# Adapter sums folded from two halves into one operand, and three steps of a fused kernel put in another order

## What is computed

```
x = x + einsum('bct,bcd->bdt', x, w0[itok_B_1_198])
x = x + einsum('bct,bcd->bdt', x, w1[itok_B_0_7])
x = x + einsum('bct,bcd->bdt', x, w2[itok_B_0_7]) + bias[itok_B_0_7][:, :, None]
gate = x @ Wg + (x @ Ag[a]) @ Bg[a]
up   = x @ Wu + (x @ Au[a]) @ Bu[a]
h    = silu(gate) * up
x    = x + h @ Wd + (h @ Ad[a]) @ Bd[a]
```

## Time and profile before

| what | us |
|---|---|
| three runs: median (all) | 1291.2 (1290.88, 1291.2, 1292.76) |
| the profiled execution | 1289.79 |
| its span in the trace | 1288.0 |
| PE busy | 1264.9 (98%), 6236 matmuls |
| weight loads (beside PE) | 1046.2 (81%) |
| DVE busy | 936.5 (73%), 1538 instructions |
| ACT busy | 551.6 (43%), 977 |
| POOL busy | 643.7 (50%), 549 |
| DMA moved | 210.10 MB, mean 163 GB/s |

### The profile page before, as it was taken

The page is one execution under the profiler, slowest core; times in us unless marked ns, Lnnn a source line. Parts: engine busy times, 40 slices in busy tenths (PEclk is TensorE's granted clock), DMA queues, the critical chain, the costliest instruction groups (busy, mean ns, idle before and its releaser), DMA issues.

```text
span 1288.0 us, 17929 instructions
## 1 busy us (share of the span) xinstructions
PE 1264.9 (98%) x6236; PEld 1046.2 (81%) x6236; DVE 936.5 (73%) x1538; ACT 551.6 (43%) x977; POOL 643.7 (50%) x549
## 2 busy tenths in 40 slices
PE   9999999999999999999999999999999999999998
PEld 7788788888888888888888888888888888888886
DVE  7986677777687676777768667767767877676765
ACT  4644445443344344454434444444443433443331
POOL 3465555455535556644545545555553444334443
PEclk9999999999999999999999999999999999999999
DMA  6855444555965345435677434545477643232424
GB/s 202 284 185 183 139 142 133 156 156 170 368 196 172 105 132 144 145 114 155 228 300 225 154 107 151 143 132 155 143 272 259 202 115 91 72 90 93 115 66 131
DMA packets 141047, 210.10 MB, mean 163 GB/s; under 512 B 43424, under 2 KB 87712, under 8 KB 140960
## 3 DMA queue, kind: packets, MB, share of 16 engines
q1 hardware_dynamic: 118656, 138.07, 34.5%
q0 software_dynamic: 22016, 70.80, 17.4%
q10 hardware_dynamic: 288, 0.10, 0.0%
HBM read 164.89 MB, written 44.04 MB: 162 GB/s over the span
## 4 chain that ended last, share of the span: by engine, by line
PE 79%; POOL 11%; issue 4%; DVE 2%; DMA 2%; ACT 0%; SPq 0%; POOLq 0%; DVEq 0%; ACTq 0%
PE px L1519 25%; PE pd L1519 20%; PE py L1519 14%; POOL b_got L658 7%; PE pz L1519 7%; POOL h_lo L689 3%; PE pz L1536 2%; PE pv L1583 2%; PE pv L1580 2%; PE pd L1776 2%; PE py L1536 2%; PE pd L1619 1%; PE px L1536 1%; PE pd L1546 1%; PE px L1542 1%
## 5 line engine op out<-in xcount | busy, mean ns | idle before, releaser
L689 POOL TENSOR_TENSOR h_lo<-g,h_hi 128x512 fp32r<-128x512 f32 x127 | 175.1, 1380 | 317.0 <-ACT h_hi L804 315.7
L1326 DVE TENSOR_TENSOR acc<-pd,acc 128x512 f32<-128x512 f32 x252 | 168.4, 686 | 108.2 <-PE pd L1519 108.1
L658 POOL DMA_INDIRECT b_got<-b_table,idx_b x192 | 187.4, 976 | 103.0 <-PE py L1536 50.0
L1519 PE MATMUL px<-xo_hi,wg_hi 128*128 128x512 f32 x540 | 216.7, 401 | 4.0 <-ACT g L804 1.9
L1519 PE MATMUL pd<-wd_hi,h_hi 128*128 128x512 f32 x512 | 206.5, 403 | 10.9 <-POOL h_lo L689 10.9
L1194 DVE TENSOR_TENSOR wg_lo<-w_raw,wg_hi 128x512 fp32r<-128x512 f32 (+1 forms) x268 | 191.8, 718 | 27.6 <-ACT wg_hi L804 27.4
L1519 PE MATMUL px<-xo_hi,wg_lo 128*128 128x512 f32 x540 | 211.8, 392 | 0.0
L1519 PE MATMUL px<-xo_lo,wg_hi 128*128 128x512 f32 x540 | 210.4, 390 | 0.0
L804 ACT ACTIVATE wg_hi<-w_raw 128x512 fp32r<-128x512 f32 (+1 forms) x272 | 152.6, 570 | 119.9 <-PE py L1536 77.2
L1519 PE MATMUL pd<-wd_lo,h_hi 128*128 128x512 f32 x512 | 201.1, 393 | 0.0
L1519 PE MATMUL pd<-wd_hi,h_lo 128*128 128x512 f32 x512 | 200.0, 391 | 0.0
(11 more groups left out here) (290 smaller groups left out, 2367.3 us busy)
## 6 DMA issues: line engine op xcount, KB each, us to landing
w_raw<-w_gu SPq DMA_DIRECT2D x68, 512.0 KB
wd_raw<-w_dn SPq DMA_DIRECT2D x64, 256.0 KB, 3.1
xo_hi<-xops SPq DMA_DIRECT2D x21, 512.0 KB, 7.9
xo_lo<-xops SPq DMA_DIRECT2D x21, 512.0 KB, 10.6
acc<-x SPq DMA_DIRECT2D x8, 1024.0 KB, 7.1
ad_raw<-ad_table SPq DMA_DIRECT2D x16, 512.0 KB, 7.1
out<-acc SPq DMA_DIRECT2D x7, 1024.0 KB, 5.4
xops<-st_hi SPq DMA_DIRECT2D x24, 256.0 KB, 2.8
```

The costliest lines, as they stand in the source:

```text
L658: gp.indirect_dma_start(out=dst, out_offset=None, in_=rows_of, in_offset=bass.IndirectOffsetOnAxis(ap=rows.bitcast(U32), axis=0)).then_inc ...
L689: return gp.tensor_tensor(dst, src_raw, src_hi, ALU.subtract)
L1326: ins = dve.tensor_tensor(dst, pd[j][:, :], dst, ALU.add)
L1519: ins = pe.matmul(psum, w_parts[wi], x_parts[xi], start=(start and i == 0), stop=(stop and i == 2), skip_group_check=more)
```

## The change

It has four parts.

1. *Fold and two products.* ACT copies rows 64 to 127 of vacc, in two halves of 256 columns, to rows 0 to 63 of the buffers ea_one and eb_one (`v_lower`); DVE adds them to the upper rows, then masks, and v's high part is written to rows 0 to 63 of `v[:, t]`, its low part to rows 64 to 127. One matmul of that operand by Bd's high part gives high by high and low by high together; a second one by Bd's low part adds high by low (and low by low, which was left out before). So `finish` has 8 matmuls per token half where it had 12: 16 a quarter for 24, 32 fewer in all.
2. *h_low(t=0) ahead of the first three gathers* on POOL in odd units.
3. *Bd's gathers for t=0 of the last quarter* move from behind the last h_low to unit 14, those for t=1 stay at the end.
4. *load_ad ahead of the weight load and table stores* of its unit on SP. In SP's list that moves one row, in unit 4 of quarter 0, past a weight load and two stores.

```diff
@@ -448,11 +450,9 @@
 
             return up1[:, :], bd_lo[:, 0, :], bd_lo[:, 1, :]
 
-        def v_parts(q, t):
-
-            if q + 1 == QUARTERS:
-                return [u[:, g, t, 0:TOK] for g in range(2)]
-            return [v[:, 0, :], v[:, 1, :]]
+        def v_fold():
+
+            return [(slice(i * HALF, (i + 1) * HALF), flat(a[0:HC, :, :])) for i, a in enumerate((ea_one, eb_one))]
 
         def st_hi_of(lo):
 
@@ -585,6 +585,8 @@
                     store_y(q - 1, 0)
                 if b == 1 and q:
                     store_y(q - 1, 1)
+                if b >= 0 and b % AD_BLOCKS == 0 and n > 1:
+                    load_ad(q, b // AD_BLOCKS)
                 k = piece_at(q, b)
                 if k is not None and n:
 
@@ -595,8 +597,6 @@
                     if k + 1 < PIECES:
                         load_b(k + 1)
                     store_b(k)
-                if b >= 0 and b % AD_BLOCKS == 0 and n > 1:
-                    load_ad(q, b // AD_BLOCKS)
                 if b == 2 and q + 1 < QUARTERS:
 
                     sp.wait_ge(p2_mm, n)
@@ -759,15 +759,18 @@
                     ad_low(q, b // 2)
                 gathers = b % 2 and (q, b) != (QUARTERS - 1, BLOCKS - 1)
                 m, to_q = ((b + 1) // 2, q) if b + 1 < BLOCKS else (0, q + 1)
+                if (q, b) != (0, 0):
+                    h_low(q, b, 0)
                 if gathers:
                     gp.wait_ge(*piece_out(max(0, m - 1)))
                     gp.wait_ge(p3_mm, n)
                     gather_b(to_q, m, 0)
-                if (q, b) != (0, 0):
-                    h_low(q, b, 0)
                 if b == BLOCKS - 2 and q + 1 < QUARTERS:
                     for g in range(2, AD_GROUPS):
                         gather_ad(q + 1, g)
+                if b == BLOCKS - 2 and q + 1 == QUARTERS:
+                    gp.wait_ge(bdown_mm, q * QP)
+                    gather_bd(q, 0)
                 j = parts_at(q, b)
                 if j is not None:
                     gp.wait_ge(turn_hi, 2 * turns(q, j))
@@ -786,17 +789,17 @@
                         gp.wait_ge(xops_out[half], TP * (q + 1) * 64)
                     for g in range(2):
                         gather_ad(q + 1, g)
-                if b == BLOCKS - 1:
+                if b == BLOCKS - 1 and q + 1 < QUARTERS:
                     if q == 0:
                         gp.wait_ge(bd_out, 2 * 16)
                     else:
                         gp.wait_ge(bdown_mm, q * QP)
 
-                    gp.wait_ge(xops_out[0], TP * min(q + 1, QUARTERS - 1) * 64)
+                    gp.wait_ge(xops_out[0], TP * (q + 1) * 64)
                     gather_bd(q, 0)
-                    if q + 1 == QUARTERS:
-                        gp.wait_ge(p4_mm, n)
-                        gather_bd(q, 1)
+                elif b == BLOCKS - 1:
+                    gp.wait_ge(p4_mm, n)
+                    gather_bd(q, 1)
 
         @block.scalar
         def _(act):
@@ -868,12 +871,17 @@
                 act.wait_ge(summed, 2 if k == S1 else TP)
                 copy(xo_hi[:, k, :], s_raw[k]).then_inc(o_hi, 1)
 
+            def v_lower(q, t):
+                act.wait_ge(down_add, added(phase(q, SUPER - 1, t), 4))
+                act.wait_ge(v_summed, 2 * (2 * q + t))
+                for cols, home in v_fold():
+                    copy(home, vacc[HC:P, t, cols]).then_inc(v_folded, 1)
+
             def v_high(q, t):
                 act.wait_ge(v_masked, 2 * q + t + 1)
-                if q + 1 < QUARTERS:
-                    act.wait_ge(bdown_mm, q * QP + TP * t)
-
-                copy(v_parts(q, t)[0], vacc[:, t, :]).then_inc(v_hi_done, 1)
+                if q:
+                    act.wait_ge(bdown_mm, (q - 1) * QP + TP * (t + 1))
+                copy(v[0:HC, t, :], vacc[0:HC, t, :]).then_inc(v_hi_done, 1)
 
             def ua_high(q, t, m):
                 src = ((g0, up0), (g1, up1))[t][m]
@@ -930,7 +938,9 @@
                     down_high(B + 1)
                     ad_high(q, b // 2)
                 if b == -1:
+                    v_lower(q - 1, 0)
                     v_high(q - 1, 0)
+                    v_lower(q - 1, 1)
 
                 if b == 0 and q:
                     act.wait_ge(ua_done, 4 * q + 4)
@@ -1059,6 +1069,7 @@
                 if (q, b) == (0, 0):
                     b_high(piece_at(q, b))
             for t in range(2):
+                v_lower(QUARTERS - 1, t)
                 v_high(QUARTERS - 1, t)
 
         @block.vector
@@ -1329,15 +1340,18 @@
                     v_mask(q, t)
 
             def v_mask(q, t):
-                dve.wait_ge(down_add, added(phase(q, SUPER - 1, t), 4))
-                v3 = vacc[:, t, :].rearrange("p (s c) -> p s c", c=C)
-                dve.tensor_tensor(v3, v3, v_rows[:, :].unsqueeze(2).to_broadcast([P, 2 * TP, C]), ALU.mult
+
+                for i, (cols, home) in enumerate(v_fold()):
+                    dve.wait_ge(v_folded, 2 * (2 * q + t) + i + 1)
+                    dve.tensor_tensor(vacc[0:HC, t, cols], vacc[0:HC, t, cols], home, ALU.add).then_inc(v_summed, 1)
+                dve.wait_ge(v_summed, 2 * (2 * q + t + 1))
+                v3 = vacc[0:HC, t, :].rearrange("p (s c) -> p s c", c=C)
+                dve.tensor_tensor(v3, v3, v_rows[0:HC, :].unsqueeze(2).to_broadcast([HC, 2 * TP, C]), ALU.mult
                                   ).then_inc(v_masked, 1)
 
             def v_low(q, t):
                 dve.wait_ge(v_hi_done, 2 * q + t + 1)
-                hi, lo = v_parts(q, t)
-                dve.tensor_tensor(lo, vacc[:, t, :], hi, ALU.subtract).then_inc(v_done, 1)
+                dve.tensor_tensor(v[HC:P, t, :], vacc[0:HC, t, :], v[0:HC, t, :], ALU.subtract).then_inc(v_done, 1)
 
             def finish(q, t, pairs=range(TP)):
                 for j in pairs:
@@ -1605,8 +1619,6 @@
             def finish(q, t):
                 pe.wait_ge(v_done, 2 * q + t + 1)
                 pe.wait_ge(bd_got[t], (q + 1) * 4 * 16)
-                vs = v_parts(q, t)
-                bd_hi, bd_low = bd_of(q, t)
                 for j in range(TP):
                     cols = slice(j * P, (j + 1) * P)
                     if t and q + 1 < QUARTERS:
@@ -1615,9 +1627,10 @@
                         pe.wait_ge(down_add, added(phase(q, SUPER - 1, 1), 4))
 
                     more = t == 1 and q + 1 == QUARTERS
-                    for i, (vp, w) in enumerate(((vs[0], bd_hi), (vs[0], bd_low), (vs[1], bd_hi))):
-                        ins = pe.matmul(finish_bank(q, t, j)[:, :], vp[:, cols], w[:, j // 2, :],
-                                        start=(i == 0 and not more), stop=(i == 2), skip_group_check=more)
+
+                    for i, w in enumerate(bd_of(q, t)):
+                        ins = pe.matmul(finish_bank(q, t, j)[:, :], v[:, t, cols], w[:, j // 2, :],
+                                        start=(i == 0 and not more), stop=(i == 1), skip_group_check=more)
                     ins.then_inc(bdown_mm, 1)
 
 
```

More of the change, by code:

```diff
@@ L321, in cond_resid_kernel @@
         u_done = sem("u_done")
+        v_folded = sem("v_folded")
+        v_summed = sem("v_summed")
         v_masked = sem("v_masked")
```

## The result

| | before | changed | ratio (95% interval) |
|---|---|---|---|
| median of the runs, us | 1291.98 (1290.88 to 1294.22, 4 runs) | 1269.15 (1268.31 to 1271.63, 4 runs) | 0.9824 (0.9804 to 0.9844) |
| profiled execution: time, span | 1289.79, 1288.0 | 1269.07, 1267.2 | |

The change is 22.8 us faster by the medians and 20.8 by the spans. The forecast was 21.6 us less, 1269.6.

A forecast was written before the change was run, and what follows sets the result against it. The prediction took PE to bound the kernel, busy 1264.9 of 1288.0 us. Gains of 17.1 (h_lo stalls), 1.7 (products), 2.1 (ad_raw) and 0.7 (end) made 21.6 us, from 1291.2 to 1269.6, range 1264.0 to 1277.0.

The forecast's parts named there:

- Stalls for h_lo: Odd units' down phase: 31 PE waits go, 0.55 us each plus 1.9 for longer ones, 19.0 us; 17.1 kept.
- PE cannot arrive earlier there: Unit 2 of quarters 1 to 3: PE follows ACT's copy of up, so 1.9 us of the gain is given back.
- Products: Finish in quarters 0 to 2: of 24 fewer matmuls worth 5.4 us, only 1.7 us is kept.
- The step on finish(t=1): Unit 1's S2 behind finish(t=1): ACT's late copy of px leaves 0.1 of 0.91 us kept, in three quarters.
- ad_raw: Unit 4 of quarter 0: the earlier load_ad removes PE's stall, 2.1 us gained.
- Fold and mask: Quarter ends: copies and adds take 0.4 us each, hidden in quarters 0 to 2, so 0 there.
- The end: Last quarter's end: b_got stall goes, but DVE sets the end, so 0.7 us gained, bounds 0.1 to 1.3.
- eight sums of 0.69: Last quarter's end: DVE's last eight sums follow v without a gap, 5.5 us, ending at 1283.9.
- DVE idle in the last 6 us: Program end: named as a sign of being wrong; DVE was expected without a gap from v_low to the end.
- 2 us to spare: Odd units: the first three gathers, 3 us later, land by 511 at worst, 2 us before PE needs them.
- The slower rival: Gathers behind h_low land too late and PE stalls, deciding from landings of 8.7 us: 1292 to 1297; chance 0.03.
- DVE pays: Rival: moved h_low stretches DVE sums in 31 units by 1.0 us, 9.5 us given back, 1279 us; chance 0.10.

The follow-up runs named there:

- e4: The kernel before with only load_ad moved ahead of its unit's weight load and stores on SP: 1287.65 us against 1290.22, ratio 0.9981.
- a1: The changed kernel run a second time, unaltered: 1270.97 us against 1293.82 before, ratio 0.9827.
- e7: The changed kernel with the last quarter's t=0 results stored pair by pair (256 KB each) instead of one 1 MB store: 1269.72 us, ratio 0.9814.
- e9: The changed kernel with POOL's old order (h_low of t=0 behind the first three gathers) in unit 1 of quarter 0 alone: 1269.96 us, ratio 0.9817.
- e3: The changed kernel with the product by Bd's low part left out of finish, 32 products fewer again: 1268.29 us, ratio 0.9827.
- e8: The changed kernel with some DVE and ACT instructions reordered at three quarter ends, where they covered the missing products: 1265.84 us, ratio 0.9802.
- e6: The changed kernel with Bd's four gathers for t=0 of the last quarter behind the last h_low again: 1272.44 us, ratio 0.9831.
- e5: The changed kernel with all six gathers of an odd unit behind both h_low on POOL: 1284.31 us, ratio 0.9938.
- e1: The kernel before with only POOL's h_low of t=0 put ahead of the first three gathers in odd units: 1273.02 us against 1290.22, ratio 0.9868.

## Why the prediction was right

**Stalls for h_lo.** 0.55 times 31 was right in kind and a little low: 0.59 and six larger ones, 20.2 for 19.0. The step that failed is "PE cannot arrive earlier there", the 1.9 us given back in unit 2 of quarters 1 to 3. In the changed kernel the load of w_raw was issued earlier with everything else and landed in time: no loss there. It is a close race, though: the same place cost 0.8 us in e4, 0.4 twice in a1 and 0.4 in all three quarters of e7. What was given back in the changed kernel's trace was 2.1 us in quarter 0, by two causes that I had not named in their places: w_raw landing 1.9 us later behind the moved gathers (e9), and POOL's low parts put back to back beside DVE (there in e1 as in the change). The size agreed by accident; 17.1 was forecast and 18.1 came.

**Products.** 1.7 was forecast (three times the 0.6 that it names would be 1.8) and 1.4 came, against 5.4 for all 24. e3 and e8 show the reason. The step on finish(t=1) named ACT's copy of px; most of the loss (0.67 of 0.91) falls one wait earlier, on DVE's wg_lo for A11, which I had not looked at. The 0.228 us for one product held: the eight of finish(t=0) run from 351.25 to 353.06.

**ad_raw.** 2.1 forecast, 2.2 in both traces.

**Fold and mask.** Hidden in quarters 0 to 2, as said. Copies and adds took 0.40 to 0.42 us, the 0.4 assumed. At the end v is there at 1257.14, 1.70 us behind the start of the last down product, where 1.75 was forecast (1278.4 less 1276.65).

**The end.** The step "eight sums of 0.69" was too dear for DVE, since sums that wait for nothing start 0.60 us apart: DVE's part came out at 1.4 us, for 0.7. But I ended the reckoning at DVE's last sum. "What is late next" was SP's queue, which took back 1.8 us (e6, e7). The term forecast at +0.7 measured -0.4. One of the signs of being wrong that I had named, DVE idle in the last 6 us, is there: it is idle for the last 5.1.

**Late gathers.** "2 us to spare" is borne out by e5: 2.3 us more cost at most 0.23 in a unit in the middle of a quarter, and most of the 14 us at the starts. The slower rival was nearer than the landing of 8.7 us, from which it was to decide, suggests.

**DVE pays.** DVE's busy time grew by 1.25 us for each moved h_low (e1). In the place of the earlier trace rows the gate product that runs beside it takes 1.69 us for 0.69, and DVE's idle time ahead of the down sums shrinks from 2.85 to 1.28 us. Timelines of DVE, before and after:

```profile
501.24 0.69 DVE L1417 TENSOR_TENSOR g<-g,up 128x512 f32<-128x512 f32 x1
```
```profile
494.00 1.69 DVE L1431 TENSOR_TENSOR g<-g,up 128x512 f32<-128x512 f32 x1
...
497.31 1.37 DVE L1337 TENSOR_TENSOR acc<-pd,acc 128x512 f32<-128x512 f32 x2 [1.28 <-PE pd L1533]
```

The Trainium skill (SBUF — State Buffer, Who interferes with whom) has the shared port pair as an exclusive lock. The rows agree in size: 1.0 to 1.25 us more of DVE for an h_low of 1.3. The idle time was the cover; where it was missing, in unit 3 of quarter 0, PE lost 0.6 us, and 0.3 at single products of f_one in e1 and a1.

## What to carry to other kernels

When an engine issues gathers and makes an operand that the bounding engine waits for, put the operand first as soon as its input is there, and measure the gathers' room by moving them further. Removing work from the bounding engine is worth only what is left by the engines whose results come just in time: look for the next two waits, not one, and move those instructions with it. At the end of a program follow the path through the last store's issue and landing; a large transfer just ahead of small ones can cost more than the compute behind it.

## What was not expected of the hardware

- A store of 256 KB takes 0.33 to 0.40 us to issue, but up to 1.25 us when a store of 1 MB was issued 0.6 us before the first of them.
- The first 65 us vary between executions of the same code there. In the profiles of e6 and e7 the granted clock is 0.50, the level of 1.2 GHz, from 20 to 23 us and again from 61 to 64, where a1 has 1.00, the level of 2.4 GHz, throughout. Over 15 to 24 us that makes a mean of 0.81. In e7 PE had waited 1.58 us for DVE just before the first of the two stretches, and 1.54 at 59 us, where a1 waits 0.65. Timelines of PE, a1 and then e7:

```profile
18.25 3.22 PE L1672 MATMUL pd<-acc 128*128 128x512 f32 x7
```
```profile
19.68 4.50 PE L1671 MATMUL pd<-acc 128*128 128x512 f32 x6 [1.58 <-DVE acc L1208]
```

e6 and e7 are 2.7 and 2.8 us behind a1 at 60 us and 4.3 behind at 65, so at the end they are compared from the last down product on. The first profile of the changed kernel has that wait too, 1.66 us, and kept 1.00, so the wait alone does not decide; what does was not tried.
